# Cross-attention and quantised FFN on one core: half-step order of the second product, paired stores, mean weight folded into the row scales, 352 columns for GpSimd

## The reference

```python
x = x + xattn(layernorm(x), ctx)          # 8 heads, 120 context rows of 192
x = x + ffn(layernorm(x))

def ffn(x):                                # 256 -> 1024 -> 256
    h = layernorm(x, ln1_g, ln1_b)
    h = bitlinear(h, w1, b1)
    h = gelu(h)                            # exact
    h = layernorm(h, ln2_g, ln2_b)
    return bitlinear(h, w2, b2)

def bitlinear(x, w, b):
    scale_x = 127 / clip(max(abs(x)), 1e-5)            # one for each row
    scale_w = 1 / clip(mean(abs(w)), 1e-5)             # one for the weight
    qx = clip(round(x * scale_x), -128, 127) / scale_x
    qw = clip(round(w * scale_w), -1, 1) / scale_w
    return qx @ qw.T + b
```

## Time and profile before

| | us |
|---|---|
| median of 3 runs | 1011.82 (1011.65 to 1012.08) |
| the profiled execution, its own time | 1012.12 |
| its span in the trace | 1010.4 |
| busy: PE, DVE, ACT, POOL | 926.0, 906.2, 932.4, 783.4 |

### The profile page before, as it was taken

How to read it: one execution, slowest core, us unless ns; L and a number is a source line. 1 busy time by engine, 2 the same in 40 slices (tenths; PEclk the granted TensorE clock), 3 DMA queues, 4 the chain that set the end, 5 groups by cost and what they waited for, 6 DMA issues and landing times.

```text
span 1010.4 us, 26145 instructions
## 1 busy us (share of the span) xinstructions
PE 926.0 (92%) x7519; PEld 568.6 (56%) x7552; DVE 906.2 (90%) x1193; ACT 932.4 (92%) x2642; POOL 783.4 (78%) x1188
## 2 busy tenths in 40 slices
PE   9999999999999999999999888888888888888887
PEld 7666666666666666666666533344444444444435
DVE  3688888888888888888888899999999999999997
ACT  5789999999999999999998789999999999999996
POOL 2476666787667666677767588999999999999996
PEclk9999999999999999999999969999999999999999
DMA  5668887777786666666586425878878777777785
GB/s 154 166 183 191 182 181 160 167 171 156 154 167 170 172 168 169 171 164 167 159 162 146 114 64 83 127 132 126 126 126 126 126 126 126 126 126 126 127 127 94
DMA packets 243888, 146.74 MB, mean 145 GB/s; under 512 B 183896, under 2 KB 201816, under 8 KB 243824
## 3 DMA queue, kind: packets, MB, share of 16 engines
q1 hardware_dynamic: 234176, 129.03, 58.5%
q0 software_dynamic: 8640, 15.73, 12.2%
q10 hardware_dynamic: 1008, 1.18, 0.3%
HBM read 71.36 MB, written 33.63 MB: 104 GB/s over the span
## 4 chain that ended last, share of the span: by engine, by line
PE 56%; POOL 17%; issue 14%; DVE 6%; ACT 5%; POOLq 1%; DMA 0%; ACTq 0%; DVEq 0%
PE banks L1460 11%; PE banks L1446 10%; POOL nq L624 7%; PE banks L1362 6%; PE banks L1417 6%; PE banks L1406 5%; PE banks L1437 4%; POOL out L615 3%; POOL g_rq L652 3%; PE banks L1427 3%; POOL gn_high L641 2%; PE banks L1395 2%; PE banks L1431 2%; PE banks L1287 2%; DVE gn_low L877 1%
## 5 line engine op out<-in xcount | busy, mean ns | idle before, releaser
L1287 PE MATMUL banks<-w_t,h_t 128*128 128x512 bf16 x472 | 126.4, 388 | 70.3 <-DVE gn_low L877 34.9
L791 DVE TRANSPOSE_TENSOR_REDUCE nm_part<-banks 128x64 f16<-128x2048 f32 x64 | 147.6, 2307 | 0.9 <-PE banks L1362 0.7
L1083 ACT ACTIVATE probs<-banks 120x512 f32<-120x512 f32 x256 | 132.3, 602 | 14.9 <-PE banks L1395 11.4
L1144 ACT ACTIVATE g_dev<-banks,g_sum 128x1024 bf16<-128x1024 f32 x128 | 144.0, 1125 | 0.0
L1138 ACT ACTIVATE banks<-banks,h_dq 128x1024 f32<-128x1024 f32 x128 | 140.3, 1096 | 3.8 <-PE banks L1292 3.7
L1460 PE MATMUL banks<-wo_sb,o_t 128*128 128x256 f32 x512 | 135.2, 399 | 1.9 <-DVE xr L797 1.3
L1316 PE MATMUL banks<-w_t,g_t 128*128 128x256 bf16 x1024 | 133.6, 274 | 1.8 <-ACT g_t L1164 1.8
L1316 PEld LDWEIGHTS banks<-w_t,g_t 128*128 128x128 f16 x1024 | 90.2, 98 | 61.4 <-issue 51.5
L1446 PE MATMUL banks<-xt,wq_c 128*128 128x256 f32 x512 | 121.5, 380 | 0.0
L1287 PEld LDWEIGHTS banks<-w_t,h_t 128*128 (+1 forms) x504 | 48.0, 98 | 121.2 <-issue 90.6
L1460 PEld LDWEIGHTS banks<-wo_sb,o_t 128*128 128x128 f32 x512 | 87.1, 190 | 37.5 <-ACT log_sum L1072 25.4
(11 more groups left out here) (177 smaller groups left out, 2516.5 us busy)
## 6 DMA issues: line engine op xcount, KB each, us to landing
x_in<-in_x SPq DMA_DIRECT2D x64, 256.0 KB, 3.7
xt<-in_x_t SPq DMA_DIRECT2D x64, 256.0 KB, 5.1
xr<-in_x SPq DMA_DIRECT2D x64, 256.0 KB, 5.1
out<-xr SPq DMA_DIRECT2D x64, 256.0 KB, 5.3
out<-h POOLq DMA_DIRECT2D x60, 256.0 KB, 4.9
ctx_t<-in_ctx_t SPq DMA_DIRECT2D x64, 128.0 KB, 4.8
r_bc<-r_rows SPq DMA_DIRECT2D x61, 128.0 KB, 4.8
w_raw<-in_w_t SPq DMA_DIRECT2D x8, 256.0 KB, 5.4
```

The source lines that it names most:

```text
L791: dve.tensor_reduce(nm_part[:, :, 0:C * RB], blocks_p, AX.X, ALU.max, negate=True, apply_transpose=True).then_inc(max_done, 1)
L1083: act.activation(probs[:, p, j, :, :], sc_p[0:KV, j, :, :], ACT.Exp, scale=SCALE).then_inc(probs_done, 1)
L1144: act.activation(g_dev[:, t, :], u_p[t], ACT.Square, scale=-float(F), bias=g_sum[:, p, t:t + 1], accum_out=g_ssq[:, p, t:t + 1]).then_inc( ...
L1287: pe.matmul(u_p[t][:, cols], h_t[:, b, t * C + c, :], w1_t[:, c, cols], start=(c == 0), stop=False, skip_group_check=True)
```

## The change

1. PE: `rows_down(j-4, 1)` now stands where `rows_down(j-4, 0)` stood, and `rows_down(j-3, 0)` where `rows_down(j-4, 1)` stood. ScalarE's `residual` follows: tile 1 of batch j-5 in the first half of step j, tile 0 of batch j-4 in the second. The semaphore of the transposes is split by tile.
2. Stores: one DMA for two batches, issued in odd steps, with one semaphore for each pair of buffers.
3. The mean magnitude of the second weight goes into the variance's scale and bias (`ve_mul`, `ve_add`), the floor and the offset row, so `out_scale` falls away. `step_size` moves from ScalarE to GpSimd, and `variance` takes its scale and bias from memory.
4. PART goes from 304 to 352: VectorE's `centre` has 672 columns instead of 720, `part` and `gain_part` have 352.
5. More unused products at the turn: 8 + 2 + 6 + 2 + 6 + 3.

```diff
-    PART = 304
+    PART = 352
...
-                def store(b, r):
-                    pool.wait_ge(out_done, b * T + T)
-                    pool.dma_start(out[b].rearrange("(p t) n -> p t n", p=P), res[:, r, :, :],
-                                   accum_op=ALU.add).then_inc(stored[r], 16)
...
+                def store_pair(b, m):
+                    pool.wait_ge(out_done, (b + 1) * T + T)
+                    pool.dma_start(out[bass.ds(b, 2)].rearrange("b (p t) n -> p b t n", p=P), res[:, 2 * m:2 * m + 2, :, :],
+                                   accum_op=ALU.add).then_inc(stored[m], 16)
...
+                def step_size(b, r):
+                    after(pool, gr_done, b + 1)
+                    after(pool, out_done, (b - 4) * T + T)
+                    pool.wait_ge(g_maxed, b + 1)
+                    pool.tensor_tensor(g_vm[:, (r + 2) % 4, T:2 * T], g_max[:, r, :], inv_qmax[:, :], ALU.mult).then_inc(gmx_done, 1)
...
                     b = j - 6
-                    if live(b, NB):
-                        store(b, (n + 2) % 4)
-                    scales(j, n % 2)
+                    if n % 2 == 1 and live(b, NB):
+                        store_pair(b - 1, ((n + 2) % 4) // 2)
+                    step_size(j - 2, (n + 2) % 4)
+                    scales(j, n)
+                    quantise_waits(j - 2, (n + 2) % 4)
                     gain_part(j, 1, n)
                     quantise_batch(j - 2, (n + 2) % 4)
...
-                    act.activation(g_vm[:, p, 0:T], g_ssq[:, p, :], ACT.Copy, scale=1.0 / F ** 3, bias=LN_EPS).then_inc(gve_done, 1)
...
+                    act.activation(g_vm[:, n, 0:T], g_ssq[:, p, :], ACT.Identity, scale=ve_mul[:, 0:1], bias=ve_add[:, 0:1]).then_inc(gve_done, 1)
...
                     if t == 0:
-                        after(act, stored[r], (b - r) * 4)
-                    act.activation(res[:, r, t, :], y2_tiles[t], ACT.Copy, scale=g_dq[:, r, t:t + 1]).then_inc(out_done, 1)
+                        after(act, stored[r // 2], (b - r) * 4)
+                    act.activation(res[:, r, t, :], y2_tiles[t], ACT.Copy, scale=g_vm[:, (r + 2) % 4, T + t:T + t + 1]).then_inc(out_done, 1)
...
                     b = j - 5
                     gelu(j, 0, p)
                     if live(b, NB):
-                        residual(b, 0, (n + 3) % 4)
+                        residual(b, 1, (n + 3) % 4)
                     deviation(j, 0, p)
                     gelu(j, 1, p)
-                    if live(b, NB):
-                        residual(b, 1, (n + 3) % 4)
+                    if live(b + 1, NB):
+                        residual(b + 1, 0, n)
                     deviation(j, 1, p)
-                    if live(j - 2, NB):
-                        step_size(j - 2, (n + 2) % 4)
-                    variance(j, p)
+                    variance(j, p, n)
...
                     if live(j - 4, NB):
-                        rows_down(j - 4, 0, n)
+                        rows_down(j - 4, 1, n)
...
-                    if not live(j - 4, NB):
+                    if live(j - 3, NB - 4):
+                        rows_down(j - 3, 0, (n + 1) % 4)
+                    elif isinstance(j, int) and j < 3:
                         unused_products()
-                    if live(j - 4, NB):
-                        rows_down(j - 4, 1, n)
...
                 project(NB - 2, 0)
+                unused_products(6)
                 pe.wait_ge(x1_done, NB - 1)
                 project(NB - 1, 1)
+                unused_products(3)
```

More of the change, by code:

```diff
@@ L265, in xattn_ffn @@
         b_placed = sem("b_placed")
-        g_turned = [sem(f"g_turned{p}") for p in range(2)]
+        g_turned = [[sem(f"g_turned{p}_{t}") for t in range(T)] for p in range(2)]
         gdq_done = sem("gdq_done")
@@ L272, in xattn_ffn @@
         out_done = sem("out_done")
-        stored = [sem(f"stored{r}") for r in range(4)]
+        stored = [sem(f"stored{m}") for m in range(2)]
         last_max = sem("last_max")
@@ L633, in quantise_batch @@
                     else:
-                        after(pool, g_turned[r % 2], 16 * (b - r % 2))
-                    out_scale(b, r)
+                        for t in range(T):
+                            after(pool, g_turned[r % 2][t], 8 * (b - r % 2))
+                def quantise_batch(b, r):
                     for t in range(1 if isinstance(b, int) and b == NB - 3 else T):
@@ L714, in _ @@
                 steps(pool, 4, NB, FFN_L0, FFN_L1, ffn, 4, {4: lambda: split_scales(2), 5: first_parts_stored})
+                step_size(NB - 2, 2)
                 last_scales()
+                quantise_waits(NB - 2, 2)
                 quantise_batch(NB - 2, 2)
-                store(NB - 6, 2)
-                store(NB - 5, 3)
+                store_pair(NB - 6, 1)
                 pool.wait_ge(last_quant, 1)
-                out_scale(NB - 1, 3)
+                last_out_scale()
                 for b, r in ((NB - 4, 0), (NB - 3, 1)):
@@ L723, in _ @@
                     pool.tensor_tensor(xr[:, r, :, :], xr[:, r, :, :], res[:, r, :, :], ALU.add).then_inc(late_sum, 1)
-                for r in range(4):
-                    pool.wait_ge(stored[r], NB * 4 - 16)
+                for m in range(2):
+                    pool.wait_ge(stored[m], NB * 4 - 16)
             @block.vector
@@ L899, in largest_rows @@
                         dve.wait_ge(floor_set, j + 1)
-                    after(dve, gdq_done, j - 3)
+                    after(dve, gmx_done, j - 3)
                     dve.wait_ge(g_affine, j * T + T)
@@ L1149, in deviation, with variance @@
                                    bias=g_nm[:, p, t:t + 1]).then_inc(part_centred, 1)
[L1151 removed]
+                def variance(b, p, n):
                     after(act, gr_done, b - 1)
+                    if isinstance(b, int) and b == 0:
+                        act.wait_ge(mean_done, 7)
                     act.wait_ge(ssq_done, b * T + T)
[L1154 to L1159 removed]
+                    act.activation(g_vm[:, n, 0:T], g_ssq[:, p, :], ACT.Identity, scale=ve_mul[:, 0:1], bias=ve_add[:, 0:1]).then_inc(gve_done, 1)
                 def gelus_turned(b):
@@ L1306, in first_rows_up, with unused_products @@
                     last.then_inc(u_ps, 1)
+                def unused_products(count=FC):
+                    for f in range(count):
+                        pe.matmul(bank[2][:, 0:D], ident_b[:, :], w2_t[:, f, :], start=True, stop=True, skip_group_check=True)
                 def turn_gelus(b, t):
@@ L1331, in spread_offset @@
                     for t in range(T):
-                        last = pe.matmul(bank[t][:, :], ones[0:1, :], b2n_bc[0:1, t * 512:(t + 1) * 512],
+                        last = pe.matmul(bank[t][:, :], w_row[:, :], b2n_bc[0:1, t * 512:(t + 1) * 512],
                                          start=True, stop=True, skip_group_check=True)
                     last.then_inc(b_placed, 1)
-                def unused_products():
-                    for f in range(FC):
-                        pe.matmul(bank[2][:, 0:D], ident_b[:, :], w2_t[:, f, :], start=True, stop=True, skip_group_check=True)
                 def ffn(j, n):
```

84 lines of the change are left out of this document (49 added, 35 removed).

## The result

The changed kernel takes **1067.86 us** (median of 4, 1061.29 to 1071.32) against 1011.74 (1011.6 to 1012.08) for the kernel before: ratio 1.0538, 95% interval 1.0507 to 1.0569. The prediction was 1069.

The account below looks back on a forecast made before the run. VectorE, ScalarE and GpSimd, within 0.1 us of each other, were taken to bound the FFN stage. Profiled 1012.1, +59 stalled loop, -0.5 early steps, -0.4 end, -0.8 turn, -0.3 to median gave 1069; range 1022 to 1094, 8 in 10.

Parts of the forecast that it names:

- the stalled loop: FFN stage: `residual` waits for the pair's store, two steps take 14.8 instead of 12.68 us, 28 times, +59.
- The landing of a pair: Paired store in the FFN stage: 7.2 us from issue to landing, bounds 5.9 to 8.4.
- Variance to store: FFN stage: path from ScalarE's variance to GpSimd's store issue, 5.60 plus 0.21 minus 0.28, 5.53 us.
- the cover goes by two edits together: FFN stage: half-step order and paired stores together leave 5.0 us between store issue and `residual`, before more than 12.
- signs named beforehand: FFN stage: ScalarE idle some 2 us before `residual`, two steps 14 to 15.5, landing near 7, VectorE and TensorE idle.
- GpSimd's own step: FFN stage: step size replaces `out_scale` at zero cost; GpSimd ends near 6.2 us a step, between 5.98 and 6.46.
- The pair's issue: GpSimd in the FFN stage: issuing a paired store costs 1.4 us, bounds 0.94 to 1.88.
- The variance from memory: ScalarE in the FFN stage: scale and bias from memory cost 0 to 0.09 us more; ScalarE 6.27 to 6.36 a step.
- PART: FFN stage, each step: VectorE 6.34 to 6.24 us, ScalarE +0.08, GpSimd +0.21.
- The turn: Turn, 590 to 600 us: 27 added products keep the clock up, -0.8 us, bounds 0 and -2.0.
- Rivals 1 and 2: FFN stage: added half lands cheaply, about 1023, chance 0.11; pair lands within 4.9 us, 1005 to 1007, chance 0.10.
- rival 3: FFN stage: nothing waits, a full engine takes the gain; ScalarE 6.36, 1011, chance 0.03; GpSimd 6.46, 1018, chance 0.02.

Follow-up runs that it names:

- e5: Kernel before with the paired stores alone, in the old half-step order: 1011.68 us, ratio 0.999.
- e6: Kernel before with the half-step order alone, stores single: 1012.33 us, ratio 1.0.
- e9: Kernel before with the paired stores and the half-step order, nothing else of the change: 1051.53 us, ratio 1.0388.
- e2: Changed kernel with the paired store issued one step earlier, as soon as its younger batch is computed: 1026.98 us, ratio 1.0162.
- e11: Changed kernel with the pair issued one step earlier and the step size moved to the start of GpSimd's step: 1019.54 us, ratio 1.0096.
- e3: Kernel before with the five added VectorE operations in the attention stage, their results unused: 1014.67 us, ratio 1.0028.
- e7: Kernel before with PART 352 instead of 304 and nothing else: 1020.24 us, ratio 1.0072.
- e8: Kernel before with the 27 more unused products at the turn alone: 1012.73 us, ratio 0.9995.
- e4: Kernel before with only the variance's scale and bias read from memory, as constants of the same value: 1020.21 us, ratio 1.0091.
- e10: Kernel before with paired stores in the old order, step size on GpSimd at the start of its step, PART 344: 1008.66 us, ratio 0.9974.

## Why the prediction was right, step by step

**The deciding term, the stalled loop: right in place and mechanism, too large in size.** The prediction had 5.53 + 7.2 + 2.07 = 14.8 for two steps, times 28 = +59. The trace has 6.09 + 6.26 + 1.99 = 14.34. 28 x (14.34 - 12.68) = +46, and the stage grew by 48.1 in all.

- *The landing of a pair*, 7.2 with bounds 5.9 to 8.4, measured 6.1 as the median and 6.26 in the loop. The 7.2 came from 4.9 + 2.15, one store's landing among the transposes and the whole share of a second one; what the second half adds is 1.2. The other reading in the prediction, 6.2 for the last two stores at the end, was the nearer one. The Trainium skill's rule quoted in the prediction, about 2.0 us plus the bytes over 436 GB/s, is worth 3.2 us by its own figures; this trace does not agree (6.1).
- *Variance to store*, 5.53, measured 6.09. Of the 0.56, 0.3 is the second `gain_part`'s wait for the power (the row at 813.44), 0.1 the longer variance (811.66 to 812.13 where 0.37 stood), and 0.13 is `out_scale`, whose going gave back less than its 0.28.
- *That the cover goes by two edits together* is shown: e5 and e6 alone 1.0 within their intervals, e9 1.0388, and e2, which gives back the cover by the place of the store, removes it. Most signs named beforehand are there: starts that repeat after 14.3, `residual` idle for a store, TensorE and VectorE idle behind `part`. Two are smaller than named: the landing is 6.1, not near 7, and the idle time is 1.2 a wait (25.8 in 22), not some 2.

**GpSimd's own step: wrong, and hidden at first.** The step "swaps `out_scale` for a step size of the same shape: zero" failed. The step size costs 0.34 to the power, which needs its result (e2, a step without a store), and 0.14 once it is moved (e11). `out_scale` gave back 0.14 of its 0.28: from the second `gain_part` to the rounding was 1.07 before (809.00 to 810.07), 1.17 with 352 columns, and is 1.03 without it, since the rounding starts 0.1 after the instruction ahead of it has ended (813.44 + 0.93 to 814.46 in after, 809.79 + 0.19 to 810.07 before). The wait for the power that was moved ahead of the second `gain_part` was not costed and is 0.23 a step (1.25 against 1.02). The pair's issue, put at 1.4 between 0.94 and 1.88, was sized about right: 0.83 as the distance of starts (803.41 to 804.23) and 0.46 behind it, 1.3, against 0.97 for a single one. Together that is GpSimd's step of 6.56 (e2, mean of a pair of steps between stores at 802.45 and 815.57), outside the bounds of 5.98 to 6.46.

**The variance from memory: wrong.** Bounds of 0 to 0.09 were taken from a `residual` of 256 columns (0.47 busy against 0.38); measured 0.19 more (0.28 less 0.09). The `residual` has one operand from memory, its scale, and the variance has two: two times 0.09 was in the rows, and was not read from them. The Trainium skill, "ScalarE: Activation LUTs", section "What ACT_TABLE_LOAD costs", gives about 93 ns for each such operand, and this trace agrees (0.19 for two). With a longer `part` this makes ScalarE's step 6.46 in e11, above the 6.36 that was its bound. Even without any stall the change would have been slower: e11, cleared of both waits, is still at 1.0096.

**The five operations on VectorE: left out.** +3 by e3, a term that the sum put at nothing without a reason.

**PART.** VectorE's gain is as costed (0.96 busy to 0.92), ScalarE's loss too (0.43 from 811.23 to 811.66 where 0.40 stood), and GpSimd's `gain_part` went from 0.83 to 0.93. With nothing else changed that makes GpSimd the bound (e7).

**The turn.** -0.8 was expected. The clock in 590 to 600 us is 0.90 (before 0.52), but the stage starts 8 us later here, and the clock falls behind that window (0.84, 0.74): it is not kept up. e8 shows no measurable gain.

**The number: close in part by luck.** In the sum's own terms the stage was to grow by 58.5 (59 less 0.5) and grew by 48.1: 10 too much, and that is itself a difference: over 28 loops the landing was put 26 too long and the path from variance to store 16 too short. All else was to give -1.2 and gave +7.6 (8.4 ahead of the stage, 0.8 less at the end): 9 too little, +3 of it the five operations and 3.7 the waits for a load, which are 1.0 or less in the other profiles looked at. The two errors cancel, and 1069 meets 1067.86. The prediction let the stalled loop swallow all other losses of the stage, so they did not show in its sum. Taken apart by the differences of profiles, the 48.1 are +4.3 that remain in e11, mostly ScalarE's longer step, +5.5 for GpSimd's order (e2 less e11), and +38.3 for the place of the pair (after less e2; 41 by the medians).

Rivals 1 and 2 are out, since the pair lands after 6.1 us, not 5.5 or less. The full engines of rival 3 exist beneath the stall, at 6.46 (ScalarE) and 6.56 (GpSimd) where it had 6.36 and 6.46; without the stall they alone decide, at 1.0096 to 1.0162.

## What to carry to other kernels

When a buffer's reuse is moved forward and its release backward, ask for the sum of both, since each alone may be free and the two together not; and issue a paired transfer when its younger half is ready. Price an operation by the next instruction that waits for its result, and in starts, not in busy time, for a tiny one above all; and look which waits an edit moves along with it. Where three engines are within 0.1 us of each other, price every instruction added to any of them, however small: 0.19 us more a step cost e4 9 us.

## What was not expected of the hardware

- **A stall cost TensorE's clock, and that cost once more.** Before, the granted clock was 1.00 in the stage; with TensorE idle behind `centre` it is 0.91 (0.91 in e9 too, which has the same stall, and 1.00 in e2 without it), that is, part of the time at the lower of its two levels. TensorE's timeline of after, behind the stall:

```profile
812.87 1.72 PE L1307 MATMUL banks<-w_t,h_t 128*128 128x512 bf16 x4 [1.84 <-DVE gn_high L900]
...
815.48 1.89 PE L1340 MATMUL banks<-w_t,g_t 128*128 128x256 bf16 x8
```

  The same eight products take 1.05 at full clock. They and the row sum behind them end at about 817.6, and the `residual` at 817.66 starts then, with 0.78 of idle time of ScalarE that the view puts down to "issue". ScalarE's waits from 640 to 1050 us:

```profile
ACT h L1194 <- DMA out<-h: 25.8, 22, 2.1
ACT h L1194 <- issue: 6.3, 10, 0.9
ACT banks L1163 <- PE banks L1312: 3.9, 7, 0.7
```

  10.2 us stand beside the 25.8 of the stores. They are not simply added. The pair issued at 817.75 would land near 824.0 by the 6.26 above, and its `residual` at 824.44 no longer waits, since TensorE has already held the engine back. So 22 waits are listed where 28 were foreseen; how much of the 38 us is the clock's no experiment separates.
- **A listed wait is less than the delay.** At 809.67 the wait is 1.31, but the start is 1.60 behind the start before it (808.07), where 0.09 is usual (801.66 to 801.75 one step earlier): some 1.5 of delay, since the overlap of neighbouring instructions is lost too.
- **Part of a store's price comes due later.** In e10 the power, `gain_part` and `out_scale` behind a pair are 1.47, 1.34 and 0.61 busy, in the step without one 1.01, 0.91 and 0.19. Their starts hardly move: only the rounding, which starts 0.1 after the instruction ahead of it has ended, comes 0.72 behind `out_scale` instead of 0.29. The distance from a DMA issue to the next start (0.83) is thus not all that it costs GpSimd.
- **Tiny operations have very different prices.** On VectorE `w_row`, 128 elements on one partition, takes 1.28 us, the product of two columns `w_inv` 1.23, and their neighbours of one column 0.14. GpSimd's timeline of after has two operations with two inputs beside them, and each of the two ends within 0.1 us of one of these:

```profile
202.94 1.29 POOL L565 TENSOR_TENSOR xr<-xr,b_bc 128x512 f32<-128x512 f32 x1
204.19 1.27 POOL L560 TENSOR_TENSOR xr<-xr,bo_bc 128x512 f32<-128x512 f32 x1
```

  It is the same in e2 and e3. So the two may have waited for GpSimd; in none of these three do they run without that neighbour, and it is not shown.
- **A pair is cheap for the queues.** Its share of the 16 engines is 200 x 0.248 / 14 = 3.5 us against 2 x 2.15 for two single stores, and the landing 6.1 against 4.9, 1.2 us for 256 KB more.
